# Computing each channel block of the state-space projection just ahead of its own scan instead of all blocks ahead of all scans, in an eight-core layer kernel

## Chip, cores and metric

One Trainium2 chip, all 8 cores. Each core takes one of the 8 sequences of the batch and runs the same program; nothing passes between cores. The metric is the device time in microseconds (us) of the slowest core.

## What is computed

x is [8, 2048, 2048] in fp32. First comes a selective state-space layer, then a quantized feed-forward layer, each with a layer norm on its input and on its output and a residual. For the change only the first counts:

```python
x_proj = einsum('bld,ed->ble', layernorm(x), W_xproj)     # e = 2048 + 16 + 16
dt     = softplus(x_proj[..., :2048])
B_ssm, C_ssm = x_proj[..., 2048:2064], x_proj[..., 2064:]
# for every time step t, channel d, state n
h = exp(dt * A[d, n]) * h + dt * B_ssm[n] * x_t
y = sum over n of h * C_ssm[n]  +  D * x_t
x = x + layernorm(y)
```

## The kernel before

Five engines are programmed: PE (matmul), DVE (vector), ACT (scalar, functions by table), POOL, and SP, which only issues loads. The program is one list of steps. Each engine takes its own steps strictly in the order in which the Python code records them (class Sched), and waits at each for the semaphores of the steps named in `waits`. So the order in which the code is written is the order on each engine.

The core's 2048 time steps are cut into 8 chunks of 256 (`TC`, loop over `c` from L435 on). A first stage before them (up to about 1,900 us) transposes and quantizes weights, the feed-forward stages stand behind them (from about 7,420 us). One chunk does this:

1. Load and normalize 2 x 128 rows of x, transpose them on PE (L460) and copy them to `xlt` (L468): 16 channel blocks of 128 channels x 256 steps.
2. The projection: 17 blocks `eb` of output rows. SP loads 1 MB of weights into one of two halves of `wxt` (L476), PE does 16 matmuls accumulating in one PSUM bank (`xpj`, L484). For blocks 0 to 15, ACT turns the sum into softplus by two functions, Exp into `spt` (`spe`, L496) and Ln with bias 1 into `dtb` (`spl`, L502). Block 16 holds B and C, and ACT copies it to `bcb` (`bcc`, L509).
3. One DVE instruction over all 16 blocks multiplies `dtb` by `xlt` into `dxt` (L513).
4. PE spreads the 32 rows of `bcb` over 128 partitions by 32 matmuls (`bcm`, L521), and ACT copies them to `bbf` and `cbf` (`bcv`, L533).
5. Loop over 16 channel blocks `dh`. For each of 16 states `n`: ACT computes exp(dt*A) into `aub` (`aex`, L542); DVE (even n) or POOL (odd n) multiplies `dxt` by `bbf` into `aub` (`uml`, L550); DVE scans over time into `hbf` (`scan`, L560). `aub` has four slots for each. Then DVE and POOL multiply the 16 results by `cbf` into `hcb` (`hcm`, L572), DVE makes `dxx` = D*x (`dxm`, L580), PE transposes and sums the 17 pieces by 34 matmuls (`ytp`, L592 and L598), and ACT copies the result to `ybf` (`yev`, L608).
6. Normalize `ybf`, add x, store (L617 to L641).

Two things of the order matter. On ACT, `yev` of block dh stands ahead of `aex` of block dh+1, and on DVE everything of block dh stands ahead of block dh+1. In the trace an fp32 matmul with 256 columns leaves two records, a transpose leaves one.

Of the kernel before, what the change touches and what calls it, by code (L numbers as in the profile page):

```python
# [23 lines left out]
ND = D // 128  # L24
NEB = 17
# [10 lines left out]
class Sched:  # L36
# [34 lines left out]
    def opt(self, *tags):  # L71
        return [t for t in tags if t in self.tags]
# [44 lines left out]
def build_nc():  # L117
    nc = bass.Bass("TRN2", target_bir_lowering=False)
    S = Sched()
    opt = S.opt  # L120
# [26 lines left out]
    def sb(st, name, p, c, dt=F32):  # L147
# [32 lines left out]
    pb = [stack.enter_context(nc.psum_tensor(f"pb{i}", [128, 512], F32))[:, :]  # L180
          for i in range(6)]
# [31 lines left out]
    for dst, src, nm in ((ident, ident_h, "ident"), (identb, identb_h, "identb"),  # L213
# [3 lines left out]
            out=d, in_=s[:, :]), tag="ld_" + nm)  # L217

    t_e = S.comp("act", lambda e: e.activation(out=aneg, in_=app, func=AF.Exp),
                 waits=["ld_app"])  # L220
    S.comp("dve", lambda e: e.tensor_scalar_mul(aneg, aneg, -1.0),
           waits=[t_e], tag="aneg")
# [5 lines left out]
    for eb in range(NEB):  # L228
        sl = eb % 2
# [88 lines left out]
    for fs in range(NFS):  # L318
        evs_all = []
        for j in range(4):  # L320
            si = fs * 4 + j
            sl = si % 2
            lt = S.dma("sp", f"wsl{sl}", lambda e, si=si, sl=sl: e.dma_start(
                out=ws[:, sl * 4096:sl * 4096 + D],
                in_=w1_h[si * 128:(si + 1) * 128, :]),
                waits=opt(f"w1q2_{si-2}") +
                      ([] if si >= 2 else opt(f"m2_a{30+si}")),
                tag=f"w1l{si}")
            c1 = S.comp("dve", lambda e, sl=sl: e.tensor_scalar(
                out=wc1[:, 0:D], in0=ws[:, sl * 4096:sl * 4096 + D],  # L330
                scalar1=ws1v[:, 0:1], scalar2=0.5, op0=ALU.mult, op1=ALU.is_ge),
                waits=[lt, tw1] + opt(f"w1qm_{si-1}"), tag=f"w1q1_{si}")
            c2 = S.comp("dve", lambda e, sl=sl: e.tensor_scalar(
                out=wabs[:, 0:D], in0=ws[:, sl * 4096:sl * 4096 + D],
                scalar1=ws1v[:, 1:2], scalar2=0.5, op0=ALU.mult, op1=ALU.is_gt),
                waits=[c1] + opt(*(["m2_a31"] if si == 0 else ())),
                tag=f"w1q2_{si}")
            qm = S.comp("dve", lambda e: e.tensor_sub(
                wqb[:, 0:D], wc1[:, 0:D], wabs[:, 0:D]),
                waits=[c2] + opt(f"w1tp_{si-1}_{ND-1}"), tag=f"w1qm_{si}")  # L340
            for dc in range(ND):
                bank = pbf[dc % 2]
# [92 lines left out]
    for c in range(NCH):  # L435
# [21 lines left out]
        for dc in range(ND):  # L457
            bank = pb[4 + (dc % 2)]
            tt_ = S.comp("pe", lambda e, dc=dc, bank=bank: [
                e.matmul(bank[:, tt * 128:(tt + 1) * 128],  # L460
                         xc[:, tt * D + dc * 128:tt * D + (dc + 1) * 128],
                         ident[:, :], start=True, stop=True, is_transpose=True)
                for tt in range(NTT)],
                waits=[f"ln1ap{c}_{tt}" for tt in range(NTT)] + ["ld_ident"] +
                      (opt(f"xevq{c}_{dc-2}") if dc >= 2 else
                       opt(f"yev{c-1}_{ND-2+dc}_{NTT-1}")),
                n=NTT, tag=f"xtp{c}_{dc}")
            S.comp("dve", lambda e, dc=dc, bank=bank: e.tensor_copy(  # L468
                xlt[:, dc * TC:(dc + 1) * TC], bank[:, 0:TC]),
                waits=[tt_] + opt(f"xpj{c-1}_{NEB-1}", f"dxt{c-1}"),  # L470
                tag=f"xevq{c}_{dc}")

        for eb in range(NEB):
            erows = 128 if eb < 16 else 32
            sl = eb % 2
            lw = S.dma("sp", f"wxt{sl}", lambda e, eb=eb, sl=sl: e.dma_start(  # L476
                out=wxt[:, sl * ND * 128:(sl + 1) * ND * 128],
                in_=wxpt_h[eb, :, :]),
                waits=(opt(f"xpj{c}_{eb-2}") if eb >= 2 else
                       opt(f"xpj{c-1}_{16-eb}", "bar_w")),  # L480
                tag=f"wxtl{c}_{eb}")
            bank = pb[eb % 2]
            mm = S.comp("pe", lambda e, eb=eb, sl=sl, erows=erows, bank=bank: [
                e.matmul(bank[0:erows, 0:TC],  # L484
                         wxt[:, sl * ND * 128 + dc * 128:
                             sl * ND * 128 + dc * 128 + erows],
                         xlt[:, dc * TC:(dc + 1) * TC],
                         start=(dc == 0), stop=(dc == ND - 1))
                for dc in range(ND)],
                waits=[lw] + [f"xevq{c}_{dc}" for dc in range(ND)] +  # L490
                      opt(f"spe{c}_{eb-2}", f"bcc{c}_{eb-2}") +
                      ([] if eb >= 2 else
                       opt(f"spe{c-1}_{14+eb}", f"bcc{c-1}_16")),
                n=ND, tag=f"xpj{c}_{eb}")
            if eb < 16:
                e1 = S.comp("act", lambda e, eb=eb, bank=bank: e.activation(  # L496
                    out=spt[:, (eb % 2) * TC:(eb % 2 + 1) * TC],
                    in_=bank[0:128, 0:TC], func=AF.Exp),
                    waits=[mm] + opt(f"spl{c}_{eb-2}") +
                          ([] if eb >= 2 else opt(f"spl{c-1}_{14+eb}")),  # L500
                    tag=f"spe{c}_{eb}")
                S.comp("act", lambda e, eb=eb: e.activation(  # L502
                    out=dtb[:, eb * TC:(eb + 1) * TC],
                    in_=spt[:, (eb % 2) * TC:(eb % 2 + 1) * TC],
                    func=AF.Ln, bias=1.0),
                    waits=[e1] + opt(f"dxt{c-1}", f"aex{c-1}_{eb*NST+NST-1}"),
                    tag=f"spl{c}_{eb}")
            else:
                S.comp("act", lambda e, bank=bank: e.activation(  # L509
                    out=bcb[0:32, 0:TC], in_=bank[0:32, 0:TC], func=AF.Copy),  # L510
                    waits=[mm] + opt(f"bcm{c-1}_31"), tag=f"bcc{c}_{eb}")

        S.comp("dve", lambda e: e.tensor_mul(dxt, dtb, xlt),  # L513
               waits=[f"spl{c}_{eb}" for eb in range(16)] +
                     [f"xevq{c}_{ND-1}"] + opt(f"uml{c-1}_255"), tag=f"dxt{c}")

        for k in range(32):
            half, n = divmod(k, 16)
# [17 lines left out]

        for dh in range(ND):
            hb0 = 0
            for n in range(NST):
                g = dh * NST + n  # L540
                slot = g % 4
                at = S.comp("act", lambda e, dh=dh, g=g, slot=slot: e.activation(  # L542
                    out=aub[:, slot * TC:(slot + 1) * TC],
                    in_=dtb[:, dh * TC:(dh + 1) * TC], func=AF.Exp,
                    scale=aneg[:, g:g + 1]),
                    waits=[f"spl{c}_{dh}", "aneg"] +
                          opt(f"scan{c}_g{g-4}", f"scan{c-1}_g{NST*ND-4+g}"),
                    tag=f"aex{c}_{g}")
                eng_u = "pool" if g % 2 == 1 else "dve"
                ut = S.comp(eng_u, lambda e, dh=dh, n=n, slot=slot: e.tensor_mul(  # L550
                    aub[:, (4 + slot) * TC:(5 + slot) * TC],
                    dxt[:, dh * TC:(dh + 1) * TC],
                    bbf[:, n * TC:(n + 1) * TC]),
                    waits=[f"dxt{c}", f"bcv{c}_{n}"] +
                          opt(f"scan{c}_g{g-4}", f"scan{c-1}_g{NST*ND-4+g}"),
                    tag=f"uml{c}_{g}")
                sw = [at, ut, "h0"] + opt(
                    f"hcm{c}_{dh-1}_{n}" if dh >= 1 else f"hcm{c-1}_{ND-1}_{n}")
                S.comp("dve", lambda e, g=g, n=n, slot=slot, hb0=hb0:
                       e.tensor_tensor_scan(  # L560
                    out=hbf[:, hb0 + n * TC:hb0 + (n + 1) * TC],
                    data0=aub[:, slot * TC:(slot + 1) * TC],
                    data1=aub[:, (4 + slot) * TC:(5 + slot) * TC],
                    initial=hst[:, g:g + 1], op0=ALU.mult, op1=ALU.add),
                    waits=sw, tag=f"scan{c}_g{g}")
# [480 lines left out]
```

How the kernel before makes its waits and increments, by code:

```python
            def run(eng_obj):  # L90
                for (eng, stream, fn, waits, inc) in per_eng[eng_name]:
                    for wtag in waits:
                        ws, wv = self.tags[wtag]
                        key = (eng_name, ws)
                        if watermark.get(key, -1) < wv:
                            eng_obj.wait_ge(sems[ws], wv)
                            watermark[key] = wv
                    insts = fn(eng_obj)
                    if insts is None:
                        insts = []
                    if not isinstance(insts, (list, tuple)):
                        insts = [insts]
                    per = 16 if stream.startswith("D") else 1
                    assert len(insts) * per == inc, (stream, len(insts), inc)
                    for i in insts:
                        i.then_inc(sems[stream], per)
```

## Time and profile before

| | us |
|---|---|
| runs: median of 2 (lowest, highest) | 11,558.99 (11,492.54, 11,625.44) |
| the profiled execution's own time | 11,483.65 |
| its span on the slowest core (core 6), first to last instruction | 11,482.0 |
| span of the fastest core (core 0) | 11,417.1 |
| busy: PE, DVE, ACT, POOL | 5,039.8, 5,406.6, 2,532.2, 1,903.0 |

No engine is busy for even half of the span, so the time is made of work that waits for other work. All starts below are microseconds from the start of the span. The granted clock (PEclk) is given as a share of the full TensorE clock: 1.00 is 2.4 GHz and 0.50 is 1.2 GHz.

### The profile page before, as it was taken

Reading aid. Unit: us, or ns where it says so; the run is one execution under the profiler, and the core shown is the slowest. Engines: PE = TensorE matmul, PEld = TensorE weight load, DVE = VectorE, ACT = ScalarE, POOL = GpSimd, SP = SyncE. Lnnn points to the kernel's source line nnn. Section 1 sums busy time; section 2 is a strip of 40 time slices with the busy share of each in tenths; the row PEclk is TensorE's granted clock in tenths of the full one; section 3 lists DMA queues with packets and bytes.
Section 4 is the critical chain, followed back from the end, with each engine's and each line's share of the span. In section 5 each row is a group of like instructions: output and inputs, shape, how many; then the busy total and the mean of one; then the engine's idle time right before and its main releaser. Section 6 shows DMA issues by size and latency. Waiting matters only on the chain.

```text
span 11482.0 us, 84780 instructions; the slowest of 8 cores (11417.1 to 11482.0 us)
## 1 busy us (share of the span) xinstructions
PE 5039.8 (44%) x21976; PEld 3016.4 (26%) x21976; DVE 5406.6 (47%) x7116; ACT 2532.2 (22%) x6860; POOL 1903.0 (17%) x2469
## 2 busy tenths in 40 slices
PE   2023335316162251614316152115999622288880
PEld 1011113215151241413315141102333211133330
DVE  1034552673737647375573737775444465500003
ACT  1543442221212222121221212211111122200000
POOL 0000000341414324142341414300111000000000
PEclk5555556667675676766667675557999855599995
DMA  6854443002020010201002020011222222244455
GB/s 219 298 198 154 176 169 138 19 8 77 0 84 0 37 48 0 85 0 63 22 4 81 0 85 0 20 39 62 86 86 87 80 103 106 102 165 161 161 168 170
DMA packets 131091, 1022.88 MB, mean 89 GB/s; under 512 B 16386, under 2 KB 16642, under 8 KB 45442
## 3 DMA queue, kind: packets, MB, share of 16 engines
q1 hardware_dynamic: 91060, 781.51, 19.9%
q0 software_dynamic: 39568, 235.96, 5.1%
q8 instruction: 199, 3.26, 0.1%
q14 instruction: 264, 2.16, 0.1%
HBM read 781.47 MB, written 235.93 MB: 89 GB/s over the span
## 4 chain that ended last, share of the span: by engine, by line
PE 40%; DVE 25%; DMA 11%; issue 11%; ACT 10%; SPq 1%; DVEq 0%; ACTq 0%; POOL 0%; POOLq 0%
PE pb L484 9%; PE pb L776 8%; PE pb L950 8%; DVE hcb L572 7%; PE pb L592 6%; DVE hbf L560 6%; ACT aub L542 5%; DMA wsl<-w 3%; PE pb L782 2%; DMA gr<-g_s 2%; PE pb L521 2%; PE pbf L343 1%; ACT stg L396 1%; DVE mb L893 1%; DVE xq2b L899 1%
## 5 line engine op out<-in xcount | busy, mean ns | idle before, releaser
L560 DVE TENSOR_TENSOR_SCAN hbf<-aub,hst 128x256 f32<-128x256 f32 x2048 | 1638.3, 839 | 1084.2 <-ACT aub L542 988.4
L592 PE MATMUL pb<-identT,hcb 128*128 128x128 f32 x4096 | 743.0, 358 | 3172.6 <-DVE dxx L580 3122.7
L592 PEld LDWEIGHTS pb<-identT,hcb 128*128 128x128 f32 x4096 | 692.2, 193 | 3203.1 <-issue 3203.1
L550 POOL TENSOR_TENSOR aub<-dxt,bbf 128x256 f32<-128x256 f32 x1024 | 787.3, 773 | 3180.5 <-DVE hbf L560 1730.5
L542 ACT ACTIVATE aub<-dtb,anegT 128x256 f32<-128x256 f32 x2048 | 982.4, 506 | 699.6 <-DVE hbf L560 602.8
L484 PE MATMUL pb<-xlt,wxt 128*128 128x256 f32 (+1 forms) x4352 | 1014.1, 400 | 5.8 <-DVE xlt L468 5.4
L950 PE MATMUL pb<-wq2s,xq2r 128*128 128x512 bf16 x4096 | 905.0, 382 | 179.9 <-DMA xq2r<-xq2t_s 179.9
L572 POOL TENSOR_TENSOR hcb<-hbf,cbf 128x256 f32<-128x256 f32 x1024 | 895.0, 906 | 448.5 <-DVE hst L566 448.5
L776 PE MATMUL pb<-wq1s,xq1t 128*128 128x512 bf16 x4096 | 930.8, 381 | 0.0
L484 PEld LDWEIGHTS pb<-xlt,wxt 128*128 128x128 f32 (+1 forms) x4352 | 856.8, 197 | 162.4 <-issue 11.7
L572 DVE TENSOR_TENSOR hcb<-hbf,cbf 128x256 f32<-128x256 f32 x1024 | 827.6, 876 | 23.2 <-DVE hst L566 22.4
L985 DVE BATCH_NORM_STATS2 bnst<-y2r 128x6 f32<-128x512 f32 x64 | 39.6, 681 | 1240.8 <-DMA y2r<-y_s 1240.8
L950 PEld LDWEIGHTS pb<-wq2s,xq2r 128*128 128x128 bf16 x4096 | 397.2, 98 | 704.3 <-issue 241.2
L608 ACT ACTIVATE ybf<-pb 128x128 f32<-128x128 f32 x256 | 57.3, 275 | 2206.0 <-PE pb L598 2205.9
L776 PEld LDWEIGHTS pb<-wq1s,xq1t 128*128 128x128 bf16 x4096 | 379.6, 98 | 618.7 <-issue 196.4
L906 PE MATMUL pbf<-identbT,xq2b 128*128 128x128 bf16 x1024 | 226.7, 265 | 698.0 <-DVE xq2b L899 542.8
L795 DVE BATCH_NORM_STATS2 gbn<-gb 128x6 f32<-128x512 f32 x256 | 177.8, 694 | 712.1 <-ACT gb L789 712.1
L513 DVE TENSOR_TENSOR dxt<-dtb,xlt 128x4096 f32<-128x4096 f32 x8 | 35.4, 4426 | 968.7 <-ACT dtb L502 968.7
L550 DVE TENSOR_TENSOR aub<-dxt,bbf 128x256 f32<-128x256 f32 x1024 | 470.4, 459 | 26.9 <-ACT bbf L533 26.9
L343 PE MATMUL pbf<-identbT,wqb 128*128 128x128 bf16 x1024 | 228.7, 265 | 414.1 <-ACT stg L350 235.6
L912 ACT ACTIVATE stg<-pbf 128x128 bf16<-128x128 bf16 x1024 | 237.1, 276 | 736.2 <-PE pbf L906 728.8
L789 ACT ACTIVATE gb<-pb,dq 128x512 f32<-128x512 f32 x256 | 175.9, 687 | 999.2 <-PE pb L782 969.7
(142 smaller groups left out, 5508.7 us busy)
## 6 DMA issues: line engine op xcount, KB each, us to landing
wxt<-wxpt_s SPq DMA_DIRECT2D x136, 1024.0 KB, 5.2
wsl<-w SPq DMA_DIRECT2D x128, 1024.0 KB, 5.2
wsl<-w SPq DMA_DIRECT2D x64, 2048.0 KB, 8.7
xq2r<-xq2t_s SPq DMA_DIRECT2D x64, 2048.0 KB, 8.8
g_s<-gb POOLq DMA_DIRECT2D x256, 256.0 KB, 2.3
gr<-g_s SPq DMA_DIRECT2D x64, 1024.0 KB, 4.8
wq1t_s<-stg POOLq DMA_DIRECT2D x16, 2048.0 KB, 7.7
wq2t_s<-stg POOLq DMA_DIRECT2D x16, 2048.0 KB, 7.0
```

The source lines that it names most:

```text
L343: tp = S.comp("pe", lambda e, dc=dc, bank=bank: e.matmul(bank[:, 0:128], wqb[:, dc * 128:(dc + 1) * 128], identb[:, :], start=True, stop=T ...
L484: e.matmul(bank[0:erows, 0:TC], wxt[:, sl * ND * 128 + dc * 128: sl * ND * 128 + dc * 128 + erows], xlt[:, dc * TC:(dc + 1) * TC], start=( ...
L521: bm = S.comp("pe", lambda e, k=k, bank=bank: e.matmul(bank[:, 0:TC], repl[0:32, k * 128:(k + 1) * 128], bcb[0:32, 0:TC], start=True, stop ...
L542: at = S.comp("act", lambda e, dh=dh, g=g, slot=slot: e.activation(out=aub[:, slot * TC:(slot + 1) * TC], in_=dtb[:, dh * TC:(dh + 1) * TC ...
L550: ut = S.comp(eng_u, lambda e, dh=dh, n=n, slot=slot: e.tensor_mul(aub[:, (4 + slot) * TC:(5 + slot) * TC], dxt[:, dh * TC:(dh + 1) * TC], ...
L560: e.tensor_tensor_scan(out=hbf[:, hb0 + n * TC:hb0 + (n + 1) * TC], data0=aub[:, slot * TC:(slot + 1) * TC], data1=aub[:, (4 + slot) * TC: ...
L572: S.comp(eng_h, lambda e, n=n, hb0=hb0: e.tensor_mul(hcb[:, n * TC:(n + 1) * TC], hbf[:, hb0 + n * TC:hb0 + (n + 1) * TC], cbf[:, n * TC:( ...
L592: e.matmul(bank[:, tt * 128:(tt + 1) * 128], hcb[:, n * TC + tt * 128: n * TC + (tt + 1) * 128], ident[:, :], start=(n == 0), stop=False, ...
L776: e.matmul(bank[:, 0:512], xq1t[:, dc * T + tb * 128:dc * T + (tb + 1) * 128], wq1s[:, sl * ND * 512 + dc * 512: sl * ND * 512 + (dc + 1) ...
L782: e.matmul(bank[:, 0:512], idr1[0:1, tb * 128:(tb + 1) * 128], b1r[0:1, fs * 512:(fs + 1) * 512], start=False, stop=True)],
L912: ev = S.comp("act", lambda e, fc=fc, bank=bank: e.activation(out=stg3[:, fc * 128:(fc + 1) * 128], in_=bank[:, 0:128], func=AF.Copy), wai ...
L950: e.matmul(bank[:, 0:512], xq2r[:, sl * NFC * 128 + fc * 128: sl * NFC * 128 + (fc + 1) * 128], wq2s[:, fc * 512:(fc + 1) * 512], start=(f ...
```

## The change

The loop over 17 projection blocks becomes a function `emit_xpj(eb, p)`, called once with block 16 where the loop stood, and once with block `dh` at the head of each turn of the loop over channel blocks. The one product `dxt` over 4096 columns becomes 16 products over 256 columns, each at the head of its turn. `p` is the place in the new order (0 for block 16, dh+1 for block dh) and now picks the half of `wxt`, the PSUM bank and the half of `spt`; the waits name the steps that stood in that place before.

```diff
-        for eb in range(NEB):
+        def emit_xpj(eb, p):
             erows = 128 if eb < 16 else 32
-            sl = eb % 2
+            sl = p % 2
+            if p >= 2:
+                pw = opt(f"xpj{c}_{16 if p == 2 else p - 3}")
+            else:
+                pw = opt(f"xpj{c-1}_{15 - p}", "bar_w")
             lw = S.dma("sp", f"wxt{sl}", lambda e, eb=eb, sl=sl: e.dma_start(
...
-            bank = pb[eb % 2]
+            bank = pb[p % 2]
...
-        S.comp("dve", lambda e: e.tensor_mul(dxt, dtb, xlt),
-               waits=[f"spl{c}_{eb}" for eb in range(16)] +
-                     [f"xevq{c}_{ND-1}"] + opt(f"uml{c-1}_255"), tag=f"dxt{c}")
+        emit_xpj(16, 0)
...
         for dh in range(ND):
             hb0 = 0
+            emit_xpj(dh, dh + 1)
+            S.comp("dve", lambda e, dh=dh: e.tensor_mul(
+                dxt[:, dh * TC:(dh + 1) * TC],
+                dtb[:, dh * TC:(dh + 1) * TC],
+                xlt[:, dh * TC:(dh + 1) * TC]),
+                waits=[f"spl{c}_{dh}", f"xevq{c}_{dh}"] +
+                      opt(f"uml{c-1}_{dh*NST+NST-1}"), tag=f"dxt{c}_{dh}")
             for n in range(NST):
...
-                    waits=[f"dxt{c}", f"bcv{c}_{n}"] +
+                    waits=[f"dxt{c}_{dh}", f"bcv{c}_{n}"] +
```

On PE, from the transposes of x in chunk 0 on, before (L484 the projection, L521 the spreading of B and C, L592 and L598 the transposes of a channel block's results):

```order
L460 MATMUL pb<-identT,xc 128x128 x32
L484 MATMUL pb<-xlt,wxt 128x256 x256
L484 MATMUL pb<-xlt,wxt 32x256 x16
L521 MATMUL pb<-bcb,replT 128x256 x32
L592 MATMUL pb<-identT,hcb 128x128 x16
L598 MATMUL pb<-identT,dxx 128x128
L592 MATMUL pb<-identT,hcb 128x128 x16
L598 MATMUL pb<-identT,dxx 128x128
```

The same place on PE now (the lines have moved: L492 the projection, L525 the spreading, L603 and L609 the transposes of a block's results):

```order
L460 MATMUL pb<-identT,xc 128x128 x32
L492 MATMUL pb<-xlt,wxt 32x256 x16
L525 MATMUL pb<-bcb,replT 128x256 x32
L492 MATMUL pb<-xlt,wxt 128x256 x16
L603 MATMUL pb<-identT,hcb 128x128 x16
L609 MATMUL pb<-identT,dxx 128x128
L603 MATMUL pb<-identT,hcb 128x128 x16
L609 MATMUL pb<-identT,dxx 128x128
L492 MATMUL pb<-xlt,wxt 128x256 x16
L603 MATMUL pb<-identT,hcb 128x128 x16
L609 MATMUL pb<-identT,dxx 128x128
```

The 16 matmuls of block 1 stand behind the transposes of block 0's results, and so on for each later block; block 0's stand behind the spreading.

On ACT, from the copy of B and C on, before (L542 the 16 Exps of a channel block, L608 the copies of its result):

```order
L509 ACTIVATE bcb<-pb 32x256
L533 ACTIVATE bbf<-pb 128x256 x16
L533 ACTIVATE cbf<-pb 128x256 x16
L542 ACTIVATE aub<-dtb,anegT 128x256 x16
L608 ACTIVATE ybf<-pb 128x128 x2
L542 ACTIVATE aub<-dtb,anegT 128x256 x16
```

The same on ACT now (L501 and L507 are the softplus's Exp and Ln, L553 the 16 Exps, L619 the copies of the result):

```order
L515 ACTIVATE bcb<-pb 32x256
L537 ACTIVATE bbf<-pb 128x256 x16
L537 ACTIVATE cbf<-pb 128x256 x16
L501 ACTIVATE spt<-pb 128x256
L507 ACTIVATE dtb<-spt 128x256
L553 ACTIVATE aub<-dtb,anegT 128x256 x16
L619 ACTIVATE ybf<-pb 128x128 x2
L501 ACTIVATE spt<-pb 128x256
L507 ACTIVATE dtb<-spt 128x256
L553 ACTIVATE aub<-dtb,anegT 128x256 x16
```

The softplus of block 1 stands between the copies of block 0's result and the 16 Exps of block 1. On DVE, the product into `dxt` of a block stands between L580 (`dxx`) of the block before and the first L561 (`uml`) of its own.

## Rows read from the trace of the kernel before

**Rows 1.** The page: busy time of the engines, and the chain that ended last.

```profile
PE 5039.8 (44%) x21976; PEld 3016.4 (26%) x21976; DVE 5406.6 (47%) x7116; ACT 2532.2 (22%) x6860; POOL 1903.0 (17%) x2469
...
PE 40%; DVE 25%; DMA 11%; issue 11%; ACT 10%; SPq 1%; DVEq 0%; ACTq 0%; POOL 0%; POOLq 0%
```

**Rows 2.** The page's costliest groups: the projection's matmuls and the product into dxt.

```profile
L484 PE MATMUL pb<-xlt,wxt 128*128 128x256 f32 (+1 forms) x4352 | 1014.1, 400 | 5.8 <-DVE xlt L468 5.4
...
L513 DVE TENSOR_TENSOR dxt<-dtb,xlt 128x4096 f32<-128x4096 f32 x8 | 35.4, 4426 | 968.7 <-ACT dtb L502 968.7
```

**Rows 3.** Timeline of one chunk's projection (start us, us, engine, line; idle before, releaser).

```profile
5369.66 127.43 PE L484 MATMUL pb<-xlt,wxt 128*128 128x256 f32 x544 [0.68 <-DVE xlt L468]
...
5379.89 0.38 ACT L496 ACTIVATE spt<-pb 128x256 f32<-128x256 f32 x1 [23.07 <-PE pb L484]
...
5483.25 0.38 ACT L496 ACTIVATE spt<-pb 128x256 f32<-128x256 f32 x1 [6.33 <-PE pb L484]
...
5490.16 0.38 ACT L496 ACTIVATE spt<-pb 128x256 f32<-128x256 f32 x1 [6.02 <-PE pb L484]
5490.64 0.42 ACT L502 ACTIVATE dtb<-spt 128x256 f32<-128x256 f32 x1
5491.22 4.43 DVE L513 TENSOR_TENSOR dxt<-dtb,xlt 128x4096 f32<-128x4096 f32 x1 [121.71 <-ACT dtb L502]
```

**Rows 4.** Timeline of one turn of the loop over channel blocks.

```profile
5165.60 0.81 DVE L580 TENSOR_SCALAR dxx<-xlt,dppT 128x256 f32<-128x256 f32 x1
5166.22 1.64 POOL L550 TENSOR_TENSOR aub<-dxt,bbf 128x256 f32<-128x256 f32 x2
5166.33 0.94 DVE L550 TENSOR_TENSOR aub<-dxt,bbf 128x256 f32<-128x256 f32 x1
...
5166.66 3.65 PE L592 MATMUL pb<-identT,hcb 128*128 128x128 f32 x16 [24.74 <-DVE dxx L580]
...
5172.36 0.27 PE L598 MATMUL pb<-identT,dxx 128*128 128x128 f32 x1
5172.73 0.45 ACT L608 ACTIVATE ybf<-pb 128x128 f32<-128x128 f32 x2 [17.27 <-PE pb L598]
5173.06 2.68 ACT L542 ACTIVATE aub<-dtb,anegT 128x256 f32<-128x256 f32 x6
5173.74 1.39 DVE L560 TENSOR_TENSOR_SCAN hbf<-aub,hst 128x256 f32<-128x256 f32 x2 [6.47 <-ACT aub L542]
5175.05 0.40 DVE L550 TENSOR_TENSOR aub<-dxt,bbf 128x256 f32<-128x256 f32 x1
5175.27 0.76 POOL L550 TENSOR_TENSOR aub<-dxt,bbf 128x256 f32<-128x256 f32 x1 [7.42 <-DVE hbf L560]
```

**Rows 5.** Two scans timed apart: beside a POOL product, and without one.

```profile
5175.55 1.02 DVE L560 TENSOR_TENSOR_SCAN hbf<-aub,hst 128x256 f32<-128x256 f32 x1
...
5526.16 0.75 DVE L560 TENSOR_TENSOR_SCAN hbf<-aub,hst 128x256 f32<-128x256 f32 x1 [26.73 <-ACT aub L542]
```

**Rows 6.** PE in short windows (window, length, PE busy, PEclk, DMA share, GB/s).

```profile
5170.00:5170.50 0.50, 0.50 (x4) 0.50 0.00 0
...
5171.00:5171.50 0.50, 0.50 (x7) 1.00 0.00 0
...
5374.00:5375.00 1.00, 1.00 (x4) 0.50 0.00 0
...
5376.00:5377.00 1.00, 1.00 (x6) 1.00 0.00 0
...
5383.00:5384.00 1.00, 1.00 (x6) 0.81 0.97 401
...
5482.20:5489.70 7.50, 7.50 (x37) 1.00 0.66 276
```

**Rows 7.** The end of the spreading of B and C, timeline, and a window over it.

```profile
5524.48 0.63 PE L521 MATMUL pb<-bcb,replT 32*128 32x256 f32 x1
...
5502.50:5525.00 22.50, 22.50 (x50) 12.06 (x49) 0.00 (x0) 9.57 (x25) 0.00 (x0) 0.50 0.00 0
```

**Rows 8.** The same product on DVE without loads and during them; the wxt loads.

```profile
5332.31 2.29 DVE L638 TENSOR_TENSOR r1b<-ybf,r1b 128x2048 f32<-128x2048 f32 x1 [0.17 <-DVE ybf L632]
...
5345.32 2.29 DVE L638 TENSOR_TENSOR r1b<-ybf,r1b 128x2048 f32<-128x2048 f32 x1 [5.42 <-DMA r1b<-x]
...
5340.70:5352.00 11.30, 0.00 (x0) 0.00 (x0) 5.28 (x8) 0.59 (x2) 0.53 (x1) 0.50 0.98 355
...
wxt<-wxpt_s SPq DMA_DIRECT2D x136, 1024.0 KB, 5.2
```

**Rows 9.** Core 0: its projection in the same chunk, and its span.

```profile
5319.26 119.73 PE L484 MATMUL pb<-xlt,wxt 128*128 128x256 f32 x544 [0.68 <-DVE xlt L468]
...
core 0: 11417.1 us, clock 0.674
```

More of the change, by code:

```diff
@@ L469, in build_nc @@
                 xlt[:, dc * TC:(dc + 1) * TC], bank[:, 0:TC]),
-                waits=[tt_] + opt(f"xpj{c-1}_{NEB-1}", f"dxt{c-1}"),
+                waits=[tt_] + opt(f"xpj{c-1}_15", f"dxt{c-1}_{dc}"),
                 tag=f"xevq{c}_{dc}")
-        for eb in range(NEB):
+        def emit_xpj(eb, p):
             erows = 128 if eb < 16 else 32
-            sl = eb % 2
+            sl = p % 2
[3 more added lines that the diff above has]
+                pw = opt(f"xpj{c-1}_{15 - p}", "bar_w")
             lw = S.dma("sp", f"wxt{sl}", lambda e, eb=eb, sl=sl: e.dma_start(
@@ L478, in build_nc @@
                 in_=wxpt_h[eb, :, :]),
-                waits=(opt(f"xpj{c}_{eb-2}") if eb >= 2 else
-                       opt(f"xpj{c-1}_{16-eb}", "bar_w")),
-                tag=f"wxtl{c}_{eb}")
-            bank = pb[eb % 2]
+                waits=pw, tag=f"wxtl{c}_{eb}")
+            bank = pb[p % 2]
+            if p >= 3:
+                bw = opt(f"spe{c}_{p-3}")
+            elif p == 2:
+                bw = opt(f"bcc{c}_16")
+            else:
+                bw = opt(f"spe{c-1}_{15-p}")
             mm = S.comp("pe", lambda e, eb=eb, sl=sl, erows=erows, bank=bank: [
@@ L489, in build_nc @@
                 for dc in range(ND)],
[L490 to L493, printed above, removed]
+                waits=[lw] + [f"xevq{c}_{dc}" for dc in range(ND)] + bw,
                 n=ND, tag=f"xpj{c}_{eb}")
             if eb < 16:
-                e1 = S.comp("act", lambda e, eb=eb, bank=bank: e.activation(
-                    out=spt[:, (eb % 2) * TC:(eb % 2 + 1) * TC],
+                e1 = S.comp("act", lambda e, eb=eb, p=p, bank=bank: e.activation(
+                    out=spt[:, (p % 2) * TC:(p % 2 + 1) * TC],
                     in_=bank[0:128, 0:TC], func=AF.Exp),
@@ L501, in build_nc @@
                     tag=f"spe{c}_{eb}")
-                S.comp("act", lambda e, eb=eb: e.activation(
+                S.comp("act", lambda e, eb=eb, p=p: e.activation(
                     out=dtb[:, eb * TC:(eb + 1) * TC],
-                    in_=spt[:, (eb % 2) * TC:(eb % 2 + 1) * TC],
+                    in_=spt[:, (p % 2) * TC:(p % 2 + 1) * TC],
                     func=AF.Ln, bias=1.0),
-                    waits=[e1] + opt(f"dxt{c-1}", f"aex{c-1}_{eb*NST+NST-1}"),
+                    waits=[e1] + opt(f"dxt{c-1}_{eb}",
+                                     f"aex{c-1}_{eb*NST+NST-1}"),
                     tag=f"spl{c}_{eb}")
```

## Prediction, made before the result

> **What bounds the kernel now.** I read the page's engine line and its chain first. No engine is busy for half the span, and the chain that ended last is made of PE for 40% and DVE for 25% [rows 1]: PE and DVE take turns and seldom work together. Next, the costliest groups, to find whose turn the change touches. The projection's matmuls take 1,014.1 us in 8 chunks, and behind them stands the product into dxt, before which DVE sat idle for 968.7 us in total [rows 2]. So in each chunk some 121 us pass in which PE projects and DVE does nothing. The timeline of one chunk shows it: PE runs 127.43 us without a gap, and DVE's product starts at 5491.22 after an idle time of 121.71 [rows 3].
>
> Then one turn of the loop over channel blocks [rows 4], where the projection will now stand. DVE ends its last instruction at about 5166.4, PE transposes from 5166.66 to 5172.63, ACT copies from 5172.73 and only then gives the first Exp of the next block, and DVE's first scan starts at 5173.74 after 6.47 us of idle time. So there is a second, smaller place where DVE waits for PE, once per channel block. In the rest of the turn, about 24.7 us, PE is idle, as the 24.74 behind its first transposes say [rows 4].
>
> **Where the projection lands.** Beside those 24.7 us it would cost nothing. But the order of the changed program puts the 16 matmuls of block dh+1 behind the transposes of block dh on PE, and PE takes its steps in order. The transposes are released by dxx, the last DVE instruction of block dh [rows 4]. So the matmuls start when DVE has nothing left, and what DVE has next, the product into dxt of block dh+1, waits for Exp and Ln, which wait for these matmuls. The change moves the work out of a long wait of DVE into 16 short ones, all still waits. Only ACT's two copies run beside it.
>
> **What is removed.** Of 17 projection blocks ahead of the scans, 16 go. The one left starts at the low clock like the first block does now, which took from 5369.66 to its reader's start at 5379.89, 10.2 us [rows 3]. With 8 chunks: 1,014.1 - 8 x 10.2 = 932.5 us saved. The big product into dxt costs nothing now: it ends at 5495.65, while block 16 is still on PE up to 5497.1 [rows 3], so removing it saves nothing. Its 16 small parts are on the path, and are counted below.
>
> **What is added for a block dh = 1 to 15** (120 in all). The copy of the result starts at 5172.73, 0.10 us behind PE's last record. With the matmuls in between, the softplus's Exp starts one block and 0.1 us later. A block at full clock takes 6.91 us (5483.25 to 5490.16 [rows 3]): Exp at 5179.75. Ln starts 0.48 later and takes 0.42, end 5180.65. The hand to DVE takes 0.16 (5491.06 to 5491.22 [rows 3]). The product into dxt is of the size of uml, 0.40 [rows 4]: to 5181.21. The first uml of the block, which before ran during the transposes, now comes behind it: 0.10 + 0.40, and 0.10 to the scan: 5181.81. Before, 5173.74: 8.07 us more. ACT's first Exp needs only Ln and is ready earlier.
>
> POOL's two first products (1.64 together) also ran during the transposes [rows 4]. They now start with the block and lie beside the first two scans. A scan beside a POOL product takes 1.02, one alone 0.75 [rows 5], so about 0.3 for each: 0.6. The bounds of this are 0 (POOL is through in time) and 1.15: where POOL gets in ahead, the DVE uml takes 0.94 and not 0.40 [rows 4]. I take 0.6, since both are released by one instruction, and at 5175.05 DVE's product started 0.22 ahead of POOL's and kept its 0.40 [rows 4]. Sum: 8.7 x 120 = 1,044 us.
>
> **At which clock these matmuls run** is the largest unknown. Within a block's transposes the granted clock is 0.50 (1.2 GHz) at 5170.0 and 1.00 (2.4 GHz) at 5171.0, after 4 us of work; in the projection it rose at 5376, after 6 us [rows 6]. The new matmuls follow the transposes without a gap: their load (5.2 us to landing [rows 8]) is released by the block two places earlier, a whole turn before. So PE comes to them at full clock. The bounds of a block are 6.91, and twice that, 13.8, at the low clock throughout; I take 6.91, by the rows at 5482 (1.00).
>
> **For block 0** (8 in all) the matmuls come behind the spreading of B and C. PE was busy for all of 5502.5 to 5525 there at 0.50 [rows 7], so the low clock is where it starts, and it takes 10.2 us. It starts one record's 0.45 behind the last at 5524.48 [rows 7], about 5524.9; Exp at 5535.1; with the same 2.06 to the scan, 5537.2 against 5526.16 now [rows 5]: 11.0, and 0.6 for POOL: 11.6 x 8 = 93 us.
>
> **Costed at nothing.** Weight loads: 17 per chunk before and after, now one in each turn and during scans. A DVE product took 2.29 us both without loads and with 355 GB/s arriving [rows 8], so I expect no slower scans. On SP's queue the loads of x for the residual stand behind the last weight load, which now goes out some three turns (over 90 us) before the chunk's end; they are needed after it, so this has cover. Exp and Ln follow each other within 0.1 us [rows 3], so no table is loaded between them.
>
> **Sum.** 1,044 + 93 - 932.5 = 204 us more, on the profiled execution's 11,483.65: 11,688, rounded to 11,690, +1.8%. This execution lies 75 us under the median of the two runs and 9 under the lower one. Core 0 as a check: its projection takes 119.73 us per chunk [rows 9], so 8 x (119.73 - 10.2) = 876 saved, 1,137 added, 11,417.1 + 261 = 11,678. Both dies end close together.
>
> Two rules of the Trainium skill bear on this, one for each side. Its page Perfetto Trace Analysis (section Optimization Strategy) says that where the busiest engine changes from regime to regime, interleaving the regimes may help beside optimizing each. By it the change should gain; this trace and the order of the queues make it an interleaving without overlap, and the first rival below is what it would give. TensorE: Matmul & The Clock Gate (section Seeing it yourself) says that a die whose cores run dense matmuls together is held at 13/16 of the clock while the load lasts. By it the new matmuls would run at 0.81, the second rival. The trace agrees in part: core 6 shows 0.81 at 5383, 7 us after its clock rose, but 1.00 at 5482, in the same unbroken load [rows 6].
>
> **The rivals.**
> - *The overlap works* (faster). If the matmuls ran beside the scans, of a turn's addition only Exp, Ln, dxt and the order behind them would be left, 2 us or less: 11,483.65 - 932.5 + 93 + 120 x 1.5 = about 10,820. For it: PE is free for 24.7 us in each turn. Against it: the PE order. Chance 0.03.
> - *The 0.81 clock* (slower). All cores now give bursts of 13 us of matmuls, and a block at 0.81 takes 6.91 / 0.81 = 8.5 us: 1.6 x 120 = 192 us on top, 11,880. For it: core 6 fell to 0.81 in its long projection. Against: that came 13 us into PE's work, where a burst now ends, and core 0's 119.73 us leave no room for it beside 10.2 + 16 x 6.91 [rows 9]. From an eighth of the matmuls at 0.81 on (23 of 192 us) the 2% line is passed. Chance 0.10.
> - *The low clock* (slower). If the rise does not come in the transposes or does not hold, 6.9 x 120 = 828 on top, 12,520. For it: PE worked 22.5 us at 0.50 during the spreading [rows 7]. Against: the rise in every kind of 128-row work seen [rows 6]. Chance 0.07.
> - *A later rise of the clock* (slower). The rise came 4 us into the transposes and 6 us into the projection [rows 6]. With turns of another length it may come 6 us in here too: 2 us more at half speed cost 1.0 a turn, 120, 11,810; from 0.2 us a turn on the 2% line is passed. Chance 0.12.
> - *POOL gets in first* (slower): 0.55 x 120 = 66 on top, 11,755, by the row of 0.94 [rows 4]. Chance 0.08.
>
> **How the numbers follow.** My forecast has 0.60, of which 0.05 lies over the 2% line. Two per cent is about what a measurement of this kernel can tell from no change; the line on top is 11,713. So faster 0.03, within 2% 0.55, slower 0.10 + 0.07 + 0.12 + 0.08 + 0.05 = 0.42. The low end of the range is the sum without POOL's 0.6 (-77) and with block 0 at full clock (-26): 11,587, taken as 11,580. The high end takes in the 0.81 clock, 11,880, taken as 11,900; the low clock and the overlap, 0.10 together, are left out.
>
> **What would show it right or wrong.** Right: in a turn the records of the projection follow the transposes at once, PEclk 1.00, the Exp 6.9 us behind them; DVE's idle time before dxt is about 14 us, 128 times; the turn goes from 30.7 us (24.74 + 5.97 [rows 4]) to about 39.4; the spreading starts about 117 us earlier in each chunk. Wrong: projection records while DVE scans (the overlap); a pitch of 0.43 and not 0.22 us between its records (low clock); DVE idle for a load; scans slower throughout a turn; or another length of the feed-forward stages, whose code is unchanged.

## The result and the profile after

| | before | after |
|---|---|---|
| median of the runs | 11,511.23 (10 runs) | 11,675.19 (11 runs) |
| span of the profiled execution, core 6 | 11,482.0 | 11,676.9 |
| spans of all cores | 11,417.1 to 11,482.0 | 11,641.1 to 11,676.9 |

The changed kernel is slower, by a ratio of 1.014 (95% interval 1.0108 to 1.0172), and stays within the 2% that the forecast took as hard to tell from no change. The forecast was 11,690 us, +1.8% on the profiled execution, in a range of 11,580 to 11,900; that execution's span grew by 194.9 us, 1.7%. Some executions of any version have a lower granted clock on the cores of one die or of both and take some per cent longer; the ratios leave these out.

The page of the changed kernel: the engine line, the chain, and the groups that answer to [rows 1, 2].

```profile
PE 5023.0 (43%) x21976; PEld 2975.8 (25%) x21976; DVE 5461.7 (47%) x7236; ACT 2557.9 (22%) x6860; POOL 1958.7 (17%) x2469
...
PE 39%; DVE 26%; issue 12%; DMA 11%; ACT 9%; POOL 1%; SPq 1%; DVEq 1%; ACTq 0%; POOLq 0%
...
L544 DVE TENSOR_TENSOR dxt<-dtb,xlt 128x256 f32<-128x256 f32 x128 | 54.5, 426 | 2084.4 <-ACT dtb L507 2084.4
...
L492 PE MATMUL pb<-xlt,wxt 128*128 128x256 f32 (+1 forms) x4352 | 996.3, 389 | 5.4 <-DVE xlt L468 5.4
```

The engines are about as busy as before, and the chain has nearly the same shares. The projection still takes 996.3 us of PE. That it is not more than before (1,014.1) is peculiar to core 6, which was at 0.81 in part of its long projection [rows 6] and is at 1.00 in the short ones; on core 0 it went from 957.7 to 994.9 us, since more blocks now start at the low clock. What moved is where DVE waits for it: 968.7 us in 8 waits became 2,084.4 us in 128. The second number is larger because the 120 waits of blocks 1 to 15 also hold the transposes of the block before, which DVE waited for before too, ahead of its first scan. The 8 waits of block 0 hold block 16 and the spreading of B and C as well; the one in the first chunk is 48.99 us.

The timeline of one turn of the changed kernel, against [rows 4]:

```profile
5159.92 0.27 PE L609 MATMUL pb<-identT,dxx 128*128 128x128 f32 x1
5160.03 7.07 PE L492 MATMUL pb<-xlt,wxt 128*128 128x256 f32 x32
5160.29 0.45 ACT L619 ACTIVATE ybf<-pb 128x128 f32<-128x128 f32 x2 [16.60 <-PE pb L609]
5167.20 0.38 ACT L501 ACTIVATE spt<-pb 128x256 f32<-128x256 f32 x1 [6.46 <-PE pb L492]
5167.67 0.42 ACT L507 ACTIVATE dtb<-spt 128x256 f32<-128x256 f32 x1
5168.19 0.43 DVE L544 TENSOR_TENSOR dxt<-dtb,xlt 128x256 f32<-128x256 f32 x1 [13.55 <-ACT dtb L507]
5168.72 0.42 DVE L561 TENSOR_TENSOR aub<-dxt,bbf 128x256 f32<-128x256 f32 x1
5168.76 2.03 POOL L561 TENSOR_TENSOR aub<-dxt,bbf 128x256 f32<-128x256 f32 x2 [14.27 <-DVE dxt L544]
5169.25 2.09 DVE L571 TENSOR_TENSOR_SCAN hbf<-aub,hst 128x256 f32<-128x256 f32 x2
...
5193.59 3.65 PE L603 MATMUL pb<-identT,hcb 128*128 128x128 f32 x16 [26.49 <-DVE dxx L591]
...
5197.24 2.65 PE L603 MATMUL pb<-identT,hcb 128*128 128x128 f32 x16
```

Read it from the top. The projection's first record starts 0.11 us behind the last transpose. ACT's copies run beside it, then ACT waits 6.46 us for it. DVE has been idle for 13.55 us when dxt starts. After the projection PE is idle for 26.49 us, while DVE scans. Nothing overlaps but the two copies. The first two scans take 2.09 us beside POOL's products, against 1.39 before [rows 4].

The granted clock at the end of that turn and in the projection behind it (window, length, PE busy, PEclk, DMA, GB/s): low in the first transposes, 2.4 GHz in the whole projection.

```profile
5193.50:5197.00 3.50, 3.41 (x16) 0.50 0.02 5
...
5200.00:5206.50 6.50, 6.50 (x31) 1.00 0.00 0
```

The turns alternate between two lengths, as the starts of the transposes show:

```profile
5233.39 3.34 PE L603 MATMUL pb<-identT,hcb 128*128 128x128 f32 x16 [26.48 <-DVE dxx L591]
...
5238.53 7.07 PE L492 MATMUL pb<-xlt,wxt 128*128 128x256 f32 x32
5272.09 3.65 PE L603 MATMUL pb<-identT,hcb 128*128 128x128 f32 x16 [26.49 <-DVE dxx L591]
...
5278.34 7.07 PE L492 MATMUL pb<-xlt,wxt 128*128 128x256 f32 x32
5311.90 3.34 PE L603 MATMUL pb<-identT,hcb 128*128 128x128 f32 x16 [26.49 <-DVE dxx L591]
```

38.70 us and 39.81 us, 39.3 on the mean. The idle time before is the same in both; from the first transpose to the projection it is 5.14 us in the one and 6.25 in the other, as the clock rises earlier or later in the transposes.

**Where the 194.9 us are.** The chunks run from the first projection record to the first load of the feed-forward stage, in the two timelines:

```profile
1917.88 126.09 PE L484 MATMUL pb<-xlt,wxt 128*128 128x256 f32 x544 [0.68 <-DVE xlt L468]
...
7421.65 10.58 SPq L666 DMA_DIRECT2D r1c<-r_s  x2
...
L950 PE MATMUL pb<-wq2s,xq2r 128*128 128x512 bf16 x4096 | 905.0, 382 | 179.9 <-DMA xq2r<-xq2t_s 179.9
```

for the kernel before, and for the changed one

```profile
1913.62 9.49 PE L492 MATMUL pb<-xlt,wxt 128*32 128x256 f32 x32 [0.68 <-DVE xlt L468]
...
1952.25 9.05 PE L492 MATMUL pb<-xlt,wxt 128*128 128x256 f32 x32
...
7594.15 96.51 SPq L677 DMA_DIRECT2D r1c<-r_s  x5
...
L961 PE MATMUL pb<-wq2s,xq2r 128*128 128x512 bf16 x4096 | 927.4, 389 | 174.7 <-DMA xq2r<-xq2t_s 174.7
```

5,503.8 us became 5,680.5: 176.7 more, where 204 were forecast. The stages behind the chunks took 22.4 us more, nearly all of it in the second feed-forward product, whose code is unchanged: its matmuls are busy for 927.4 us against 905.0 before. On core 0 they are busy for 904.3 us against 903.4, so this belongs to that execution of core 6 (mean granted clock 0.91 over the product, 0.93 before) and not to the change. The stage ahead of the chunks was 4.3 us shorter.

Core 0, whose projection was at 1.00 throughout before (6.91 us a block, where core 6 had 7.0 to 7.7), grew by 228.4 us, from 11,417.1 to 11,645.5. So with the projection at 1.00 on both sides the change costs 2.0%. Core 6 grew by less because its long projection had been held back before. That the 1.4% of the medians is less for the same reason is likely, and not shown: the other runs have no trace.

### The profile page after: what moved, and what is told of

Read it like the earlier page. It is cut to its first block, busy times and chain, and to the rows that moved or that the text cites. A ratio compares the mean times of both kernels' runs of the same rounds, so it can differ in the third digit from the quotient of the medians.

```text
span 11676.9 us, 85244 instructions; the slowest of 8 cores (11641.1 to 11676.9 us)
## 1 busy us (share of the span) xinstructions
PE 5023.0 (43%) x21976; PEld 2975.8 (25%) x21976; DVE 5461.7 (47%) x7236; ACT 2557.9 (22%) x6860; POOL 1958.7 (17%) x2469
## 4 chain that ended last, share of the span: by engine, by line
PE 39%; DVE 26%; issue 12%; DMA 11%; ACT 9%; POOL 1%; SPq 1%; DVEq 1%; ACTq 0%; POOLq 0%
PE pb L492 8%; PE pb L961 8%; PE pb L787 8%; DVE hcb L583 7%; DVE hbf L571 7%; PE pb L603 6%; ACT aub L553 3%; DMA wsl<-w 3%; PE pb L793 2%; DMA gr<-g_s 2%; PE pb L525 2%; PE pbf L343 1%; ACT stg L396 1%; DVE mb L904 1%; DVE xq2b L910 1%
## 5 line engine op out<-in xcount | busy, mean ns | idle before, releaser
L603 PE MATMUL pb<-identT,hcb 128*128 128x128 f32 x4096 | 744.8, 360 | 3394.9 <-DVE dxx L591 3368.3
L571 DVE TENSOR_TENSOR_SCAN hbf<-aub,hst 128x256 f32<-128x256 f32 x2048 | 1728.0, 883 | 109.2 <-DVE aub L561 3.2
L603 PEld LDWEIGHTS pb<-identT,hcb 128*128 128x128 f32 x4096 | 700.0, 195 | 3442.6 <-issue 3442.6
L561 POOL TENSOR_TENSOR aub<-dxt,bbf 128x256 f32<-128x256 f32 x1024 | 838.1, 823 | 3305.1 <-DVE dxt L544 1787.3
L553 ACT ACTIVATE aub<-dtb,anegT 128x256 f32<-128x256 f32 x2048 | 997.5, 505 | 836.8 <-DVE hbf L571 729.7
L544 DVE TENSOR_TENSOR dxt<-dtb,xlt 128x256 f32<-128x256 f32 x128 | 54.5, 426 | 2084.4 <-ACT dtb L507 2084.4
L961 PE MATMUL pb<-wq2s,xq2r 128*128 128x512 bf16 x4096 | 927.4, 389 | 174.7 <-DMA xq2r<-xq2t_s 174.7
L492 PE MATMUL pb<-xlt,wxt 128*128 128x256 f32 (+1 forms) x4352 | 996.3, 389 | 5.4 <-DVE xlt L468 5.4
L492 PEld LDWEIGHTS pb<-xlt,wxt 128*128 128x128 f32 (+1 forms) x4352 | 813.3, 189 | 154.4 <-issue 33.5
L619 ACT ACTIVATE ybf<-pb 128x128 f32<-128x128 f32 x256 | 57.1, 274 | 2205.0 <-PE pb L609 2204.9
L561 DVE TENSOR_TENSOR aub<-dxt,bbf 128x256 f32<-128x256 f32 x1024 | 407.6, 398 | 13.7 <-DVE dxt L544 0.5
```

Of the source, the lines that this page charges most:

```text
L492: e.matmul(bank[0:erows, 0:TC], wxt[:, sl * ND * 128 + dc * 128: sl * ND * 128 + dc * 128 + erows], xlt[:, dc * TC:(dc + 1) * TC], start=( ...
L571: e.tensor_tensor_scan(out=hbf[:, hb0 + n * TC:hb0 + (n + 1) * TC], data0=aub[:, slot * TC:(slot + 1) * TC], data1=aub[:, (4 + slot) * TC: ...
L603: e.matmul(bank[:, tt * 128:(tt + 1) * 128], hcb[:, n * TC + tt * 128: n * TC + (tt + 1) * 128], ident[:, :], start=(n == 0), stop=False, ...
L961: e.matmul(bank[:, 0:512], xq2r[:, sl * NFC * 128 + fc * 128: sl * NFC * 128 + (fc + 1) * 128], wq2s[:, fc * 512:(fc + 1) * 512], start=(f ...
```

## The experiments

Turn lengths below are means over the turns from block 1 on (120 in a kernel), from the starts in the timelines of one core. Each version was timed beside runs of the kernel before, whose median was 11,497 to 11,546 us in them.

### The projection one block earlier

```diff
-            emit_xpj(dh, dh + 1)
+            if dh == 0:
+                emit_xpj(0, 1)
+                emit_sp(0, 1)
+            if dh + 1 < ND:
+                emit_xpj(dh + 1, dh + 2)
...
+            if dh + 1 < ND:
+                emit_sp(dh + 1, dh + 2)
             hc = S.comp("dve", lambda e, dh=dh, hb0=hb0: e.tensor_copy(
```

The function `emit_sp` holds the two softplus functions, split off from `emit_xpj`.

> The changed kernel with the matmuls of block dh+1 written at the head of turn dh (on PE ahead of the transposes of block dh), and its softplus behind the 16 Exps of block dh. Theory (the projection is on the path only because it stands behind the transposes on PE): the matmuls run beside the scans, the turn goes back to about 30.7 us, DVE's idle time before dxt vanishes, and only blocks 16 and 0 are left ahead of the scans: before 11,510 - 932 + 90 = about 10,670. Rival (the addition comes from the split itself, the spread loads or contention, not from the order): DVE slows beside PE and loads, and the time stays above 11,300.

Measured: 10,648.26 us, ratio to before 0.9255 (0.9197 to 0.9314), turn 30.8 us. One turn:

```profile
5201.00 0.41 DVE L553 TENSOR_TENSOR dxt<-dtb,xlt 128x256 f32<-128x256 f32 x1
...
5206.99 7.07 PE L492 MATMUL pb<-xlt,wxt 128*128 128x256 f32 x32
...
5208.26 1.39 DVE L580 TENSOR_TENSOR_SCAN hbf<-aub,hst 128x256 f32<-128x256 f32 x2 [6.32 <-ACT aub L562]
...
5220.62 0.36 ACT L505 ACTIVATE spt<-pb 128x256 f32<-128x256 f32 x1
...
5231.94 0.41 DVE L553 TENSOR_TENSOR dxt<-dtb,xlt 128x256 f32<-128x256 f32 x1
```

The projection lies beside scans, its softplus starts with no idle time 6.6 us after the sums are ready, and dxt of the next block runs without a wait. So the same split, with matmuls and softplus earlier in the code, is worth 900 us where the change as made costs 160. Splitting, loads in the loop and PE beside DVE cost nothing that shows.

Two orders moved here at once, PE's and that of the softplus on ACT. The matmuls alone one block earlier were not run. The first rival of the prediction prices them, with the softplus left where the change has it, at about 10,820; by that estimate most of the 900 us is PE's order, and the rest is not shown apart.

### The small products alone

```diff
-        S.comp("dve", lambda e: e.tensor_mul(dxt, dtb, xlt), ...
...
+            S.comp("dve", lambda e, dh=dh: e.tensor_mul(
+                dxt[:, dh * TC:(dh + 1) * TC], ...
```

> The kernel before with only the product into dxt split into 16, each at the head of its turn; the projection stays ahead of the scans. Theory: its inputs are ready and it falls into DVE's idle time during the transposes, so no change, within 0.3% of before (11,510). Rival (the 16 small products cost by themselves): 128 x 0.5 = +60 us, 11,570.

Measured: ratio 1.0008 (0.9962 to 1.0054), whose upper end still touches the rival. The trace settles it: the turn is 30.8 us against 30.7 before, where the rival asks for 0.5 us more, and the product runs inside the wait that was there before (6.46 us now, 6.47 in [rows 4]):

```profile
5229.92 0.41 DVE L536 TENSOR_TENSOR dxt<-dtb,xlt 128x256 f32<-128x256 f32 x1
5230.26 3.65 PE L595 MATMUL pb<-identT,hcb 128*128 128x128 f32 x16 [24.75 <-DVE dxx L583]
...
5237.33 1.39 DVE L563 TENSOR_TENSOR_SCAN hbf<-aub,hst 128x256 f32<-128x256 f32 x2 [6.46 <-ACT aub L545]
```

The small products fall into idle time when their input is ready; in the changed kernel it is not.

### Half of the projection, without and with the overlap

```diff
-                         start=(dc == 0), stop=(dc == ND - 1))
-                for dc in range(ND)],
+                         start=(dc == 0), stop=(dc == ND // 2 - 1))
+                for dc in range(ND // 2)],
```

> The changed kernel with 8 of the 16 matmuls of each projection block (half of the sum over channels is left out). Theory (each matmul of the projection is wholly on the path, at full clock in turns 1 to 15): 16 records of 0.216 less in each turn, 3.46 x 120 = 415, and about 4 to 5 us less for each of the two blocks per chunk that start at the low clock, 70: 11,675 - 485 = 11,190. Rival (part of the projection is hidden, the turn grew by hand-overs): under 250 us less. If the matmuls ran at the low clock it would be 6.9 x 120, 830 less.

> The overlap version with 8 of the 16 matmuls of each projection block (half of the sum is left out). Theory (its projection is hidden in turns 1 to 15, and only blocks 16 and 0 are on the path): the turn stays at 30.8 us, and the time falls by 8 x 8 to 10 = 60 to 80 us only, to 10,580; without the overlap the same cut was worth 470. Rival (the projection still costs in each turn): 200 us or more.

Measured: 11,205.58 us (2 runs) from the changed kernel, 470 less. Its block fell from 7.07 us to

```profile
5271.75 3.62 PE L492 MATMUL pb<-xlt,wxt 128*128 128x256 f32 x16
```

and its turn from 39.3 to 36.0 us, by about the 3.46 of 16 records at full clock. From the overlap version 10,607.85 (2 runs), 40 less, somewhat under the 60 to 80 expected, with its turn where it was (30.7). The two runs lie 49 us apart; the spans of the two profiled executions differ by 53.7. So in blocks 1 to 15 the matmuls that were left out are on the path in the one, and hidden in the other.

### ACT's copies later, in three kernels

```diff
+                if dh >= 1 and n == 8:
+                    pend()
                 at = S.comp("act", lambda e, dh=dh, g=g, slot=slot: e.activation(
```

The function `pend` holds the two copies of block dh-1.

> The kernel before with ACT's two copies of block dh's result written behind the first eight Exps of block dh+1 instead of ahead of all of them. Theory (the 6.47 us in which DVE waits behind each block are only the order on ACT: the copies wait for the transposes, and the Exps stand behind them): DVE goes on into the next block, the turn falls from 30.7 to about 25 us: 5.8 x 120 = 700 less, 10,820. Rival (DVE needs the pause anyway, since scans and products beside POOL's get slower by as much, or the transposes themselves hold the buffers): under 250 us less.

> The changed kernel with the copies of block dh's result behind the first eight Exps of block dh+1, the same edit that was worth 710 to 750 us to the kernel before. Theory (in the changed kernel DVE waits for the projection behind the transposes, and the copies run beside it): no change, within 0.5% of the changed kernel, 11,675. Rival (the two waits are separate here too): 5.8 x 120 = 700 less.

> The overlap version with the copies of the result moved in the same way. Theory: the two gains are of separate waits and add up, since PE has 13 us of work in a turn of 25: 10,650 - 5.6 x 120 = 9,980. Rival (PE's transposes and projection now come late for DVE or for the softplus in the shorter turn): less than half of that, above 10,300.

Measured: on the kernel before, 10,792.44 us, ratio 0.9356 (0.9301 to 0.9411), turn 24.7 us. On the changed kernel, 11,717.02 us, 42 above it and within the 0.5% expected, and the turn is 39.3 as without it; its ratio to before is 1.0194 (1.0131 to 1.0258), which overlaps the changed kernel's own 1.0108 to 1.0172. On the overlap version, 9,969.27 us, ratio 0.8635 (0.8589 to 0.8681), turn 25.1: the fastest kernel of the study. First a turn of the kernel before with the copies moved, where DVE's scans start 0.7 us behind the transposes and not after them:

```profile
5222.19 3.65 PE L594 MATMUL pb<-identT,hcb 128*128 128x128 f32 x16 [17.88 <-DVE dxx L582]
5222.91 1.67 DVE L562 TENSOR_TENSOR_SCAN hbf<-aub,hst 128x256 f32<-128x256 f32 x2
```

Then one turn of the overlap version with the copies moved, and its busy times in that stretch (PE, PEld, DVE, ACT, POOL):

```profile
5208.60 0.41 DVE L553 TENSOR_TENSOR dxt<-dtb,xlt 128x256 f32<-128x256 f32 x1
...
5208.93 3.65 PE L616 MATMUL pb<-identT,hcb 128*128 128x128 f32 x16 [12.29 <-DVE dxx L604]
5209.12 0.42 DVE L572 TENSOR_TENSOR aub<-dxt,bbf 128x256 f32<-128x256 f32 x1
...
5209.65 2.10 DVE L582 TENSOR_TENSOR_SCAN hbf<-aub,hst 128x256 f32<-128x256 f32 x2
...
5201.00:5226.00 25.00, 13.69 (x66) 12.42 (x66) 23.79 (x36) 8.97 (x20) 13.60 (x16) 0.68 0.08 28
```

DVE is busy for 23.79 of 25 us, and its scans run beside the transposes. The kernel before had two waits of DVE for PE; both were a matter of order, on ACT and on PE. In the changed kernel the first one's cure does nothing, since the copies are through (5160.74) long before the projection is (5167.10).

### PE kept busy, with changing data and with constant data

```diff
             emit_xpj(dh, dh + 1)
+            S.comp("pe", lambda e: [
+                e.matmul(pb[2][:, 0:TC], ident[:, :], xlt[:, 0:TC], start=True, stop=True)
+                for _ in range(54)], waits=[f"bcv{c}_31"], n=54)
```

The second and third form take `pb[2][:, 0:512]`, `ones[:, 0:512]`, and 27 or 29 of them.

> The changed kernel with 54 matmuls more on PE in each turn behind the projection (128x256 fp32, into a bank nobody reads), which fill PE's idle time during the scans; no result depends on them. Theory (each turn's transposes begin at the low clock because PE was idle): they now begin at the full one and take 3.9 and not 6.3 us: 2.4 x 128 = 310 less, 11,370. Rival (continuous work brings the 0.81 clock): transposes 4.7, projection 8.5 us, and the filler ends late: no gain or slower, 11,700 and more.

> The changed kernel with 27 matmuls in PE's idle time of each turn, of the identity with a tile of ones (128x512 fp32), in place of the 54 with x: as long, but with operands that hardly change. Theory (full clock at the head of a turn is worth 2.0 us, as in the turns of the last run that kept 1.00, and the 0.81 came from the current that changing data draws): the clock stays at 1.00, the turn is 37.35 us, 2.0 x 128 = 255 less than the changed kernel, 11,420. Rival (the 0.81 comes from continuous work whatever the data): turns of 41.2 us again, 11,800 or more.

> The quiet filler with 29 matmuls in each turn instead of 27, so that PE idles 1.6 and not 3.4 us ahead of the transposes at full clock. Theory (turns above 37.35 us in the last run came from a clock that fell in the pause of 3.4 us): nearly all turns are 37.35 us, 11,440 in all. Rival (the clock falls for another reason, the 0.81 above all, and a longer filler then ends late): turns no shorter on the mean than 38.4, 11,590 or more.

The first was run four times: 11,980.91, 11,924.30, 12,013.65 and 11,650.49 us. In the first three, the cores of one die or of both have a mean granted clock of 0.75 to 0.76, and they set the time. Cores that kept 0.80, in the last three, took 11,503 to 11,536 us, some 130 less than the 11,641 to 11,677 of the changed kernel. So neither forecast holds as it stands: the filler gains where the clock stays up, less than half of the 310 forecast, and the rival's 0.81 takes more than that where it comes. No ratio is taken from it. A turn of core 0 in the profiled execution (11,980.91), and a window over it:

```profile
4039.43 8.58 PE L492 MATMUL pb<-xlt,wxt 128*128 128x256 f32 x32
4047.84 28.53 PE L545 MATMUL pb<-xlt,identT 128*128 128x256 f32 x108
...
4000.00:4040.00 40.00, 40.00 (x171) 0.81 0.00 1
```

The block takes 8.58 us and not 7.07, the filler 28.53 and not 23.47, and the turn 41.2.

With the constant operand, 27 gave 11,590.79, ratio to before 1.0065 (1.0021 to 1.0110), between the two forecasts. The clock did not stay at 1.00 there: on core 6, 27 of the 102 fillers seen whole take longer than 23.34 us, up to 27.67, and 0.81 is granted inside the matmuls of ones; on cores 4 and 5 of the same die none does. One of the long ones, and a window in it:

```profile
3371.81 27.62 PE L545 MATMUL pb<-onesT,identT 128*128 128x512 f32 x54
...
3376.00:3381.00 5.00, 5.00 (x11) 0.81 0.05 20
```

29 gave 11,426.72 (six of ten runs at 11,421 to 11,428), ratio 0.9938 (0.9903 to 0.9973); the other four took 11,530 to 11,888, with a mean granted clock down to 0.76 on the cores of a die against 0.81. Transposes after a pause of 3.35 us (27), then after 1.66 (29), and a window of the latter:

```profile
5226.70 3.44 PE L608 MATMUL pb<-identT,hcb 128*128 128x128 f32 x16 [3.35 <-DVE dxx L596]
...
5253.70 1.94 PE L608 MATMUL pb<-identT,hcb 128*128 128x128 f32 x16 [1.66 <-DVE dxx L596]
...
5240.00:5280.00 40.00, 38.34 (x132) 1.00 0.00 1
```

With the shorter pause the turns are 37.4 us and the clock stays at 2.4 GHz through whole turns. So the low clock at the head of each turn costs 39.3 - 37.4 = 1.9 us, 250 us in all. It is a detour here: with the overlap and the copies moved, DVE scans beside the transposes, and their clock is off its path.

TensorE: Matmul & The Clock Gate (section Seeing it yourself) in the Trainium skill says that the fall to 13/16 is driven by current, and that all-ones operands don't trip it. The traces agree in part only: 0.81 stood for turns on end with x as operand, and the profiled execution with 29 matmuls of ones has 1.00 through its turns, but with 27 of them the window above has 0.81 in the ones themselves. The projection works on x in every turn of both, so these runs do not set the operand apart, and that constant data keeps the clock up is not shown.

### POOL's first products left out

```diff
-                ut = S.comp(eng_u,
+                ut = at if (dh >= 1 and n in (1, 3)) else S.comp(eng_u,
```

> The changed kernel without POOL's first two products of each block from block 1 on (n = 1 and 3; those scans read what an older product left). Theory (POOL's products beside the first two scans stretch them from 1.39 to 2.09 us): the turn falls by 0.7 us, from 39.34 to 38.65, 84 us over the kernel, 11,590; the first two scans take 1.39. Rival (the scans are slow there for another reason, the arriving weights): scans stay at 2.09 and the turn at 39.3.

Measured: 11,644.45 us (2 runs), a turn of 39.0 to 39.2 on most cores. The scans did what was expected, the sum of the kernel did not:

```profile
5202.92 1.39 DVE L571 TENSOR_TENSOR_SCAN hbf<-aub,hst 128x256 f32<-128x256 f32 x2
...
5192.19 8.58 PE L492 MATMUL pb<-xlt,wxt 128*128 128x256 f32 x32
...
5192.20:5200.50 8.30, 8.30 (x34) 0.81 0.00 0
```

POOL's products cost 0.70 us a turn, as the two scans show, and where the clock held the turn shows it too: turns whose projection takes 7.07 us are 38.7 us on the mean, on each core looked at, against the 38.65 expected. But in 15 to 24 turns of a core the projection ran at 0.81, these turns are 40.6 to 40.9 us, and they gave more than half of the gain back. This is the rival of the 0.81 clock.

The changed kernel is not free of it. In its profiled execution nine blocks on each of cores 4 and 5 take 7.3 to 7.6 us and not 7.07, with a clock below 1.00 near their end:

```profile
6721.21 7.43 PE L492 MATMUL pb<-xlt,wxt 128*128 128x256 f32 x32
...
6726.00:6728.00 2.00, 2.00 (x10) 0.86 0.00 0
```

And in two of its runs (11,705.61 and 11,734.37) the cores of one die have a mean clock of 0.658 to 0.661 against 0.663 to 0.664, as in the profiled execution here (0.660 to 0.661). So nothing shows that leaving out the products brings the 0.81 on; what does was not found.

## Why the prediction was right

- *Where the projection lands.* Right, and shown from three sides: moving it by one block in the PE order, with its softplus, gives 900 us, halving it gives about 3.4 us a turn without the overlap and nothing with it, and the copies' place on ACT does not matter behind it.
- *What is removed and what block 0 adds.* Forecast, per chunk, 932.5 / 8 - 11.6 = 105 us saved at the chunk's head. Measured: 176.7 less 120 x 8.6 = 1,032 leaves -855, so 107 a chunk. The blocks that start at the low clock were a little cheaper than the 10.2 taken, 9.49 and 9.05 in the rows above.
- *What is added per turn.* Forecast 8.7, measured 39.3 - 30.7 = 8.6. By its steps: from ACT's copy to Exp 6.91 (7.02 forecast); Exp to the first scan 2.05 (2.06); the two scans 0.70 (0.6); less the 1.01 that passed from the copy to the first scan before, 8.65. POOL did start 0.04 behind DVE's product and not ahead of it, which kept its 0.42: the rival of POOL in front did not come.
- *The clock.* 1.00 in the projection, as forecast. The rise alternates between turns, but from the first start to the last end the 34 matmuls of a block's transposes take 5.93 us on the mean of all 128, and took 5.92 before, so the rival of a later rise was half true and worth nothing. The rival of the 0.81 clock came in 18 of some 960 blocks, in part of each.
- *Costed at nothing.* Right, by the overlap version, for the weight loads during scans. DVE's waits for the residual's loads of x are 38.7 us in all, 42.8 before, and no table is loaded in the chunks. The small products were counted at 0.40 on the path, and are there at 0.43; where their input is ready they cost nothing (1.0008).
- *The size.* +204 forecast for the chunks, +176.7 measured. The 27 us are 120 x 0.1 in the turns and 8 x 2 at the heads. The profiled spans differ by 194.9 only because the stages behind the chunks took 22.4 us more, so that the total of that execution (11,678.69 against the 11,688 of the sum) comes nearer than its parts is luck. So is the nearness to the median, 11,675.19: the sum was put on an execution 28 us under the median before, and between the medians there are 164 us and not 204. Core 0, forecast at +261, grew by 228.4; there too the sum is some 30 us high.

## What to carry to other kernels

Where each engine takes its steps in the order of the code, interleaving two stages hides nothing by itself: look at what stands ahead of the moved step on its own engine, and what releases that. Here the moved matmuls stood behind transposes released by DVE's last instruction, and one block earlier, with the softplus moved along, would have been right: 7% faster and not 1.4% slower. A split wait is also worth checking for what it delays beside itself, since products that ran in an idle time before (0.7 us a turn here) then run beside work that they slow.

## What was not expected of the hardware

- The turn's length went into a regular alternation of 38.7 and 39.8 us, with every other turn's clock rising later.
- With the filler of 27, PE paused for 3.25 to 3.86 us ahead of the transposes on core 5, and in 65 of 128 blocks they began at 1.2 GHz. With that of 29 the pause was mostly 1.5 to 1.9 us, and two of 128 blocks had the low clock in their first transposes, both behind a pause of 2.0.
- The 0.81 clock comes in short bursts too: with POOL's products left out a block took 8.58 us in bursts of 15 us of matmuls, and in the changed kernel some blocks took 7.3 to 7.6.
- It does not always come to a whole die: with 27 matmuls of ones, cores 6 and 7 had fillers of up to 27.7 us, and cores 4 and 5 none over 23.4.
